# Plain aggregation passes of a graph network regrouped: four tiles a group, eight groups of gathered rows, four of one-hots and sums

## The reference

```
msg = xt[row_f] * norm[:, None]
out = jax.ops.segment_sum(msg, col_f, num_segments=n)
```

## Time and profile before

| | us |
|---|---|
| median of 3 runs (lowest, highest) | 8757.37 (8740.85, 8768.17) |
| the profiled execution, its own time | 8772.01 |
| its span, first to last instruction | 8770.2 |
| first convolution pass, first gather to start of the last additions | 4273.67 to 5468.42 |
| second convolution pass, the same | 5544.27 to 6737.21 |

### The profile page before, as it was taken

The page is one execution under the profiler, slowest core; times in us unless marked ns, Lnnn a source line. Parts: engine busy times, 40 slices in busy tenths (PEclk is TensorE's granted clock), DMA queues, the critical chain, the costliest instruction groups (busy, mean ns, idle before and its releaser), DMA issues. The chain is left out here.

```text
span 8770.2 us, 97349 instructions
## 1 busy us (share of the span) xinstructions
PE 3809.7 (43%) x22250; PEld 3522.3 (40%) x22250; DVE 3289.3 (38%) x8047; ACT 2044.2 (23%) x3881; POOL 4563.5 (52%) x4487
## 2 busy tenths in 40 slices
PE   4333333463555565566433333433333433444256
PEld 2333332352555554566433333433333433333246
DVE  4222223776344443677422222322223211111375
ACT  1000000583333333798100000000000100000067
POOL 2555554350555655333366665466664355555344
PEclk8666666796566656787655555655556555555589
DMA  5555554341444444455111111111111233333234
GB/s 150 159 159 161 161 160 133 99 150 38 118 121 120 122 120 117 159 196 168 38 46 46 46 46 42 48 45 46 46 46 35 67 80 84 82 83 82 60 125 139
DMA packets 973147, 864.07 MB, mean 99 GB/s; under 512 B 350004, under 2 KB 837256, under 8 KB 972808
## 3 DMA queue, kind: packets, MB, share of 16 engines
q1 hardware_dynamic: 798344, 452.32, 17.9%
q0 software_dynamic: 159744, 356.39, 14.8%
q10 hardware_dynamic: 14976, 54.53, 1.8%
HBM read 669.20 MB, written 193.56 MB: 98 GB/s over the span
## 5 line engine op out<-in xcount | busy, mean ns | idle before, releaser
L762 POOL DMA_INDIRECT sum_rows<-tab_row,src_idx x1664 | 1569.7, 943 | 1016.8 <-issue 500.9
L387 PE MATMUL l_pK<-l_winr,l_hotT 128*128 128x128 f32 (+2 forms) x4992 | 1046.3, 376 | 2080.5 <-ACT l_hotT L429 1375.3
L387 PEld LDWEIGHTS l_pK<-l_winr,l_hotT 128*128 128x128 f32 x4992 | 1002.9, 307 | 2159.4 <-issue 1266.0
L899 DVE TENSOR_TENSOR acc<-acc,sum_pA 128x128 f32 x4160 | 990.5, 288 | 1851.8 <-DMA w_gat<-in_L_gnn_W 1535.6
L796 PE MATMUL sum_pA<-sum_hot,sum_rows 128*128 128x128 f32 x3328 | 777.9, 428 | 1619.6 <-DMA sum_rows<-tab_row,src_idx 1406.2
L796 PEld LDWEIGHTS sum_pA<-sum_hot,sum_rows 128*128 128x128 f32 x3328 | 722.0, 329 | 1675.5 <-issue 914.1
L369 POOL DMA_INDIRECT l_rows<-tab_wh,src_idx x832 | 784.9, 943 | 724.8 <-DMA spill<-l_rows 325.1
L369 POOL DMA_INDIRECT l_rows<-tab_qv,src_idx x832 | 786.5, 945 | 689.4 <-DMA spill<-l_rows 299.2
L369 POOL DMA_INDIRECT l_rows<-tab_ax,src_idx x832 | 800.7, 962 | 619.1 <-issue 248.8
L796 PE MATMUL sum_pA<-sum_hot,sum_wrow 128*128 128x128 f32 x4992 | 728.1, 306 | 354.7 <-DVE sum_hot L261 237.9
L428 ACT ACTIVATE l_hotT<-l_pT 128x512 f32<-128x512 f32 x315 | 187.4, 595 | 2875.4 <-remote 1236.2
(11 more groups left out here) (233 smaller groups left out, 4372.6 us busy)
## 6 DMA issues: line engine op xcount, KB each, us to landing
spill<-l_rows SPq DMA_DIRECT2D x312, 512.0 KB
sum_rows<-spill SPq DMA_DIRECT2D x312, 512.0 KB
l_winr<-tab_k SPq DMA_DIRECT2D x840, 64.0 KB
sum_line<-src_lo ACTq DMA_DIRECT2D x104, 512.0 KB, 3.9
l_winr<-tab_b SPq DMA_DIRECT2D x840, 32.0 KB
sum_rows<-tab_row,src_idx POOLq DMA_INDIRECT x1664
l_winr<-tab_er SPq DMA_DIRECT2D x840, 2.0 KB
l_rows<-tab_qv,src_idx POOLq DMA_INDIRECT x832
```

Source lines behind the costliest of these rows:

```text
L387: last = nc.tensor.matmul(pK[:, b, u, :], hotT[:, b, u, :], winr[:, b * TB + u, :], start=True, stop=True)
L762: nc.gpsimd.indirect_dma_start(rows[:, b * TB + u, :], None, tab_row, bass.IndirectOffsetOnAxis(src_idx[:, t:t + 1], 0)).then_inc(s_rows[b ...
L899: nc.vector.tensor_tensor(acc[:, u % 2, bass.ds(at, P)], acc[:, u % 2, bass.ds(at, P)], pA[:, b, u, :], ALU.add).then_inc(s_add, 1)
```

## The change

A new function `convolve(name)` does the two plain passes; `aggregate` stays for the other three. The tiles, the products, the additions and the gathers are the same in number, kind and order. What differs:

- a group is four tiles (`GT`), so there are 208 groups (`NG`);
- gathered rows have eight groups (`DEEP`), 32 tiles; one-hots and PSUM sums have four groups (`HOTS`), 16 tiles, as before in size;
- POOL's group n waits until group n-8 is summed;
- the order on DVE is prepare(n+2), add_windows(n); prepare(n) waits until group n-4 is summed;
- the first two `prepare` stand ahead of the clearing of `acc`;
- the loops of PE and DVE have 26 rounds of eight groups, instead of 52 rounds of two batches.

```diff
+            GT, HOTS, DEEP = 4, 4, 8
+            NG = T // GT
...
+                hot = sb(L + "hot", [P, HOTS, GT, P], fp32, cx)
+                rows = sb(L + "rows", [P, DEEP, GT, F], fp32, cx)
+                pA = ps(cx, L + "pA", [P, HOTS, GT, P])
...
+                        for n in range(NG):
+                            j = n % DEEP
+                            if n >= DEEP:
+                                pool.wait_ge(s_sum, HOTS + n - DEEP + 1)
+                            for u in range(GT):
+                                t = n * GT + u
+                                nc.gpsimd.indirect_dma_start(
+                                    rows[:, j, u, :], None, tab_row,
+                                    bass.IndirectOffsetOnAxis(src_idx[:, t:t + 1], 0)).then_inc(s_rows[j], 16)
...
+                            pe.wait_ge(s_hot, n + 1)
+                            pe.wait_ge(s_rows[j], i * (16 * GT) + 16 * GT)
+                            for u in range(GT):
+                                last = nc.tensor.matmul(pA[:, j % HOTS, u, :], rows[:, j, u, :], hot[:, j % HOTS, u, :],
+                                                        start=True, stop=True)
+                            last.then_inc(s_sum, 1)
...
+                        def prepare(n, j):
+
+                            dve.wait_ge(s_sum, n + 1)
...
+                        def add_windows(n, j):
+
+                            dve.load(regs, base[0:1, bass.ds(n * GT, GT)])
+                            dve.wait_ge(s_sum, n + HOTS + 1)
...
+                        dve.sem_inc(s_sum, HOTS)
...
+                        prepare(0, 0)
+                        prepare(1, 1)
+                        nc.vector.memset(acc[:], 0.0).then_inc(s_add, 2)
+                        with dve.Fori(0, NG // DEEP) as i:
+                            for j in range(DEEP):
+                                prepare(i * DEEP + j + 2, j + 2)
+                                add_windows(i * DEEP + j, j)
...
-        aggregate("sum2", None)
+        convolve("sum2")
         node_phase("mid")
-        aggregate("sum3", None)
+        convolve("sum3")
```

33 lines of the change are left out of this document (added).

## The result

The changed kernel takes 8,774.0 us (median of 12 runs, 8,754.7 to 8,792.9), the kernel before 8,755.9 (12 runs): a ratio of 1.0022, 95% interval 1.0013 to 1.0031. That is 18 us more, where 11 us less were forecast. The size is inside the 0.3% that the prediction called no change, the sign is not.

The account below looks back on a forecast made before the run. Bound: a server behind the gathers at 1.43 us each, no engine full. 8772.0 - 6 (longer streams) - 5.6 (pass ends) = 8760 profiled; the median lies 14.6 lower: 8,746 us. Range 8,460 to 8,800, the forecast's own 8,725 to 8,775.

Parts of the forecast that it names:

- 1.43 us a gather, whatever the ring: Convolution passes: something behind the gathers takes 1.43 us for each while POOL issues every 1.25; a pass takes 1,180 to 1,192.
- rival 1: POOL's waits: the delay has an upper end that 32 tiles cover, so more buffers hide it; 8,477 us, chance 0.21.
- one ratio at three lengths: Late signals after 16, 23 and 24 gathers: 1.426 to 1.433 us a gather each time, held against buffers hiding the delay.
- stream of 23 gathers: POOL, from 4595.45 to the late signal at 4628.31: 32.86 us, 1.429 a gather, counted from an issue gap.
- 3 us a pass for longer streams: Rows for 32 tiles: the 0.3 us pause after late signals is paid less often; gain 3 us, bounds 0 to 11.
- the last products and additions are four tiles, not eight: about 2.8 us a pass: End of each convolution pass: half of 3.78 + 1.80 is saved, about 2.8 us a pass, so 5.6.
- half as many jumps, on engines with room. 0: Loops of the convolution passes, bodies of eight groups: half as many jumps, on engines with room, gain 0.
- Streams as long or longer, each pause longer: Sign that the forecast is right: POOL's streams as long or longer, pauses longer, still 1.42 to 1.44 us a gather.
- DVE's waits of over 10 us: Sign that the forecast is right: DVE's additions in the changed passes show waits of 10 us and more.
- any stream of over 30 gathers followed by a signal at clearly less than 1.4: POOL's streams: the forecast falls if one of over 30 gathers is followed by a signal at clearly less than 1.4 us each.
- Rival 2: Lag behind the gathers stays at 5.4 us in longer streams; 59 us a pass gained, 8,634 or so, chance 0.15.
- Rival 3: One-hots hold up PE after 12 tiles, adding 3.6 us a stretch, 125 us a pass; 9,000 us, chance 0.14.

Follow-up runs that it names:

- Paced: The changed kernel with POOL clearing a 128x128 scratch tile behind each gather of the convolution passes; ratio to the kernel before 1.0021.
- paced_more: The changed kernel with POOL clearing a 128x256 scratch tile behind each gather of the convolution passes; ratio to the kernel before 1.0053.
- far64: The changed kernel with row buffers for 52 groups (208 tiles), gathering rows of 64 elements, so its sums are wrong; 8,798.2 us, ratio 1.0184.
- after_again: The changed kernel once more, unaltered, on the chip of the follow-up runs; ratio to the kernel before 1.0023.
- before_again: The kernel before once more, unaltered, one run for a trace from the chip of the follow-up runs; convolution passes 1,199.4 and 1,198.1 us.
- eights: The changed kernel with groups of eight tiles, two one-hots and sums, and row buffers for four groups (32 tiles); ratio to the kernel before 0.9996.
- closest pair: The kernel before and the changed kernel, each with POOL clearing a 128x256 scratch tile behind each score-pass gather; 8,333.0 and 8,351.1 us.
- ring16: The changed kernel with row buffers for sixteen groups of four tiles (64 tiles) instead of eight groups; ratio to the kernel before 1.0046.
- before_plus80: The kernel before with 80 more semaphore instructions on DVE at the start of the second convolution pass; 7,583.8 us, ratio 1.0020.
- after_plus75: The changed kernel with 75 more semaphore instructions on DVE at the start of the second convolution pass; 7,539.5 us, ratio to the kernel before 0.9963.

## Why the prediction was right and wrong

**Right: the bound and its size.** 1.43 us a gather, whatever the ring: 70 streams of 20, all but six of them at 1.429 to 1.437 (the six at 1.36 to 1.40), passes of 1,187 us from first to last gather (forecast 1,180 to 1,192). Doubling the rows did not remove the waits. Paced, paced_more and far64 show this as the cause, and not as an arithmetic accident; the argument against rival 1, one ratio at three lengths, carried. Its stream of 23 gathers was counted from an issue gap; from the pause before, at 4582.45, it is 32 gathers in 45.86 us, 1.433, so nothing hangs on that choice.

**Wrong: 3 us a pass for longer streams.** The streams became shorter, and from first to last gather the passes take 0.5 and 2.8 us more in the first profiles, 0.9 and 0.2 less in after_again against before_again: nothing was gained that can be told from 0. So 6 us of the forecast's sum were not there. Only eights ends its gathers 3.0 us sooner, for a reason that is not shown.

**Wrong: "the last products and additions are four tiles, not eight: about 2.8 us a pass".** This is the failed step that turned the sign of the passes. It takes the end of a pass from the work of the last group, as if DVE were up to date. It holds where signals are prompt (2.3 us). Where they are held, DVE has all the groups before it that POOL was allowed to issue: 24 to 32 additions in the changed kernel, 8 to 16 in the one before. From the release to the last addition the changed kernel takes 4 to 8 us longer, where 2.8 less were forecast; a whole pass takes 2 to 7 us more, by the pair of kernels that is compared. The earlier trace rows had the clue: the additions that start at 6734.73 had 9.4 us of waiting behind them, and more rows let more of them wait. I used the lag for the rate only, and not for what lies behind it when the gathers stop.

**Wrong: "half as many jumps, on engines with room. 0".** The other failed step, and nearly as large as both passes together. No cost of the changed loops' own jumps shows; but their longer bodies move all of DVE's code behind them, and a loop that DVE bounds, in another stage, pays 10.8 us (327.9 instead of 317.1). No row of the convolution passes could show that. The trace of before does hold a sign: the first and the last weighted pass that are scaled by heads run the same code, and take 329.7 and 317.2 us. The loop of the first lies from 308 to 368 and holds 320.

**The sum by what was measured:** +6.2 and +6.6 for the passes in the first profiles (4.5 and 2.2 in the closest pair) and +10.8 for the last weighted pass. That is 17.5 to 23.6, for a difference of 18.2 in the medians. The untouched score passes take 1,307 to 1,332 us on like chips from one kernel to the next, and in the first two profiles the three together are 13.1 us shorter in the changed kernel, so single profiles do not add up to a few us.

**The signs that I named.** "Streams as long or longer, each pause longer": shorter ones (20) with shorter pauses (3.6), at the same ratio. DVE's waits of over 10 us are there, and PE waits for one-hots that lie behind a late signal, 1,280.2 us. My own test, "any stream of over 30 gathers followed by a signal at clearly less than 1.4", is met by the first stream of each pass: 48 gathers in 65.6 and 63.4 us, 1.37 and 1.32. It does not refute the rate: a single signal got through, 4 more gathers went out, and 52 gathers took 73.4 us, 1.41. While POOL is ahead some signals come through, and the ratio holds only for the one that ends the lag.

**The rivals.** Rival 1 is what happens on chips without the lag, where it needs no more buffers than before. Rival 2 (the lag stops growing) is true at 30 us, which only far64 reached, and then POOL itself is slowed. Rival 3 was the right sign with another place: not a chain after each stream, but one after the last.

The Trainium skill (Perfetto Trace Analysis, Identifying Performance Opportunities) says that a repeating gap can mean too few buffers. Here ring16 has four times the rows of the kernel before, keeps the gaps and is slower: the runs decide against it.

## What to carry to other kernels

Where an engine issues faster than something behind it can serve, more buffers move the wait and make a longer tail; measure the rate over several stream lengths, and try slowing the issuer to just above it. In the score passes, where a chain of engines waits for the late signals, 0.33 us of idle work behind each gather made this kernel 3.5% faster; in the convolution passes, where nothing but the rate was to be had, the same work cost 13 to 15 us a pass (paced_more against after_again). Both were run only on chips with the lag. When a run-ahead is given more room, cost the end of the stage by all that may be waiting then, not by the last item. And before you credit or blame an edit for 0.1%, look at the stages that it does not touch: unrolling moves the loops behind it.

## What the runs showed of the hardware

- A gather costs 1.42 to 1.43 us on some chips whatever its rows (64 or 128) and bytes (256 to 1,024 a row), though POOL issues it in 1.25. POOL can be some 21 gathers, 30 us, ahead (far64); then many of its gathers take 1.0 to 1.8 us instead of 0.94. On other chips there was no such rate.
- While POOL is ahead, signals to POOL, VectorE and ScalarE are late, by 9.4 us in the kernel before and up to 19 in far64, and SyncE's transfers are slow (15.6 us for eight instead of 4.35). At 1.445 us a gather both are prompt (paced_more: additions 0.35 us after the products).
- A loop of 61 instructions on DVE costs 0.20 us more a round where it holds an instruction with a number 64 over a multiple of 128, counted over the recorded instructions as here (317.1 against 327.9 us for 51 rounds; before_plus80, after_plus75).
- On the chips without the lag POOL pauses 1.8 us more than usual at every 112th gather, in the kernel before and in all score passes, but not in the changed convolution passes.
